# Cross attention of a decoder layer: probabilities normalised before the turn, turned output summed in place, scores a tile ahead, weights stored split

## The reference

```
x = x + self_attention(layernorm(x))
x = x + cross_attention(layernorm(x), ctx)
x = x + ffn(layernorm(x))
```

```
scores  = qh @ kh.T / sqrt(dk)
weights = softmax(scores)
out     = weights @ vh
```

## Time and profile before

| | us |
|---|---|
| median of 3 runs (lowest, highest) | 3618.52 (3617.93, 3620.3) |
| the profiled execution | 3618.95 |
| its span | 3616.8 |
| TensorE busy (share of the span) | 3440.5 (95%) |
| VectorE busy | 1494.1 (41%) |
| ScalarE busy | 1185.0 (33%) |
| GpSimd busy | 1250.3 (35%) |
| mean granted TensorE clock | 0.977 |

### The profile page before, as it was taken

The page is one execution under the profiler, slowest core; times in us unless marked ns, Lnnn a source line. Parts: engine busy times, 40 slices in busy tenths (PEclk is TensorE's granted clock), DMA queues, the critical chain, the costliest instruction groups (busy, mean ns, idle before and its releaser), DMA issues. The chain is left out here.

```text
span 3616.8 us, 49438 instructions
## 1 busy us (share of the span) xinstructions
PE 3440.5 (95%) x18100; PEld 2677.0 (74%) x18100; DVE 1494.1 (41%) x2238; ACT 1185.0 (33%) x1679; POOL 1250.3 (35%) x563
## 2 busy tenths in 40 slices
PE   6999999999999999999999679989979999998999
PEld 5888887888878888878787467767767777763587
DVE  3232332323332232423232446656656665652453
ACT  3232232323233232323222235445444454440110
POOL 4334343434324343434342334434334443320000
PEclk9999999999999999999999889999999999999999
DMA  4323233323333232332221254544555455534032
GB/s 168 106 94 113 89 135 130 115 93 106 127 128 117 93 110 93 128 134 89 85 93 53 108 150 128 173 146 137 156 152 137 129 161 162 141 88 157 35 133 76
DMA packets 137253, 431.16 MB, mean 119 GB/s; under 512 B 24112, under 2 KB 24112, under 8 KB 137144
## 3 DMA queue, kind: packets, MB, share of 16 engines
q1 hardware_dynamic: 131384, 408.58, 35.1%
q10 hardware_dynamic: 5760, 20.97, 1.4%
HBM read 316.21 MB, written 37.75 MB: 98 GB/s over the span
## 5 line engine op out<-in xcount | busy, mean ns | idle before, releaser
L446 POOL TENSOR_TENSOR sa_wl<-sa_wraw,sa_wh 128x1024 fp32r<-128x1024 f32 x192 | 458.2, 2402 | 777.3 <-ACT sa_wh L597 777.3
L53 PE MATMUL sa_u<-sa_ln_xh,sa_wh 128*128 128x512 f32 x1536 | 628.5, 409 | 4.4 <-DVE sa_ln_xl L254 4.4
L54 PE MATMUL sa_u<-sa_ln_xl,sa_wh 128*128 128x512 f32 x1536 | 599.7, 390 | 0.0
L55 PE MATMUL sa_u<-sa_ln_xh,sa_wl 128*128 128x512 f32 x1536 | 599.3, 390 | 0.0
L457 POOL TENSOR_TENSOR sa_pl<-sa_praw,sa_ph 128x1024 fp32r<-128x1024 f32 x128 | 318.0, 2516 | 446.4 <-ACT sa_ph L649 446.4
L53 PE MATMUL sa_pr<-sa_ph,sa_oh 128*128 128x512 f32 x1024 | 428.6, 419 | 0.1
L746 DVE TENSOR_TENSOR sa_acc<-sa_pr,sa_acc 128x512 f32<-128x512 f32 x256 | 176.9, 692 | 569.3 <-PE sa_pr L55 569.3
L54 PE MATMUL sa_pr<-sa_pl,sa_oh 128*128 128x512 f32 x1024 | 400.8, 391 | 0.0
L55 PE MATMUL sa_pr<-sa_ph,sa_ol 128*128 128x512 f32 x1024 | 400.0, 391 | 0.0
L738 DVE TENSOR_TENSOR sa_ol<-sa_o,sa_oh 128x512 fp32r<-128x512 f32 x128 | 88.6, 692 | 718.5 <-ACT sa_oh L661 718.5
L53 PEld LDWEIGHTS sa_u<-sa_ln_xh,sa_wh 128*128 128x128 f32 x1536 | 289.3, 188 | 83.6 <-issue 24.2
(11 more groups left out here) (185 smaller groups left out, 5765.7 us busy)
## 6 DMA issues: line engine op xcount, KB each, us to landing
sa_wraw<-in_wqkv SPq DMA_DIRECT2D x192, 512.0 KB, 3.5
sa_praw<-in_wproj SPq DMA_DIRECT2D x128, 512.0 KB, 3.5
ca_wraw<-w_folded SPq DMA_DIRECT2D x96, 512.0 KB, 3.2
ca_kstack<-ca_kmh SPq DMA_DIRECT2D x256, 128.0 KB, 2.4
ca_wraw<-in_wo SPq DMA_DIRECT2D x33, 512.0 KB, 4.2
ca_kstack<-ca_kml SPq DMA_DIRECT2D x128, 128.0 KB, 2.4
ca_qstack<-ca_qh SPq DMA_DIRECT2D x256, 64.0 KB, 2.5
...
```

The costliest lines, as they stand in the source:

```text
L53: nc.tensor.matmul(out, ah, bh, start=(first and i == 0), stop=False)
L54: nc.tensor.matmul(out, ah, bl, start=False, stop=False)
L55: ins = nc.tensor.matmul(out, al, bh, start=False, stop=(last and i == len(parts) - 1))
L446: nc.gpsimd.tensor_tensor(wl[:, u % 3], wraw[:, u % 3], f32(wh[:, u % 3]), ALU.subtract).then_inc(w_split, 1)
```

## The change

In self-attention the folded weights are stored as two arrays, high and low: `copy_fold` writes the high part and VectorE the low part (`low_fold`), and `store_fold` issues two DMAs. The cross phase loads both straight into `wh` and `wl`; only Wo's slice is still split there.

In the attention the negated, scaled maximum goes to ScalarE as the exp's bias: 8 exps of 128 columns a tile, from the scores' bank, which is free only after the last of them. VectorE sums each half of the slots and inverts the sums (`sums`), GpSimd multiplies (`normal_probs`), and the normalised probabilities are turned. v stands in pairs of slots with zeros between (`VW` = 96), so that the two slots of a pair, one into rows 0 to 15 of a band of 32, the other into rows 16 to 31, are summed in one place by `mix_values`; the result is the output, turned, as `project` wants it. copy_oT, turn_oT, scale_o and turn_o are gone. scores(t) stands before turn_probs(t - 1).

The diff, cut:

```diff
-                        act.wait_ge(fold_stored, m * 16 + 16)
-                    nc.scalar.activation(fold[:, half * HALF:(half + 1) * HALF], v_ps[:], ACT.Copy
-                                         ).then_inc(v_copied, 1)
+                        act.wait_ge(fold_stored, m * 32 + 32)
+                    nc.scalar.activation(foldh[:, half * HALF:(half + 1) * HALF], v_ps[:], ACT.Copy
+                                         ).then_inc(fold_hi, 1)
 
                 def store_fold():
                     if not s.steady:
                         return
                     act.wait_ge(v_copied, v0 + 4)
-                    act.dma_start(tile_of(w_folded, m), fold[:]).then_inc(fold_stored, 16)
+                    act.dma_start(tile_of(w_folded_hi, m), f32(foldh[:])).then_inc(fold_stored, 16)
+                    act.dma_start(tile_of(w_folded_lo, m), f32(foldl[:])).then_inc(fold_stored, 16)
...
+                def low_fold(half):
+                    if not s.steady:
+                        return
+                    dve.wait_ge(fold_hi, m * 2 + (half + 1))
+                    cols = slice(half * HALF, (half + 1) * HALF)
+                    nc.vector.tensor_tensor(foldl[:, cols], v_ps[:], f32(foldh[:, cols]), ALU.subtract
+                                            ).then_inc(v_copied, 1)
...
                 low_o(0)
                 next_moments(0)
+                low_fold(0)
                 low_o(1)
                 next_moments(1)
                 add_projected(0)
+                low_fold(1)
...
-        v = sb("ca_v", [P, TILES * SLOTS, DP])
+        v = sb("ca_v", [P, TILES * PAIRS, VW])
...
-            def weights(n, item, g, skipped=0):
-
-                if not (isinstance(n, int) and n < 0):
-                    sp.wait_ge(w_split, splits(n, item + (-2), skipped))
-                src = {OUT: wo, VALUE: w_folded, KEY: w_folded, QUERY: w_folded}[item]
-                first = {OUT: 0, VALUE: 2 * CH, KEY: CH, QUERY: 0}[item]
-                sp.dma_start(wraw[:, item % 2], tile_of(src, g + first)).then_inc(wraw_loaded[item % 2], 16)
+            def weights(u, g):
+                first = CH * WHICH[u]
+                sp.dma_start(f32(wh[:, u]), tile_of(w_folded_hi, g + first)).then_inc(w_loaded[u], 16)
+                sp.dma_start(f32(wl[:, u]), tile_of(w_folded_lo, g + first)).then_inc(w_loaded[u], 16)
+
+            def next_weights(s, u):
+                if s.nxt:
+                    sp.wait_ge(u_done, s.n * U + (u + 1))
+                    weights(u, s.next_g)
...
-                    weights(s.n + 1, OUT, s.g, 0 if s.nxt else 2)
+                    next_weights(s, 0)
+                    sp.wait_ge(ow_split, s.n + 1)
+                    sp.dma_start(owraw[:], tile_of(wo, s.g)).then_inc(owraw_loaded, 16)
...
-                    if s.nxt:
-                        weights(s.n + 1, VALUE, s.next_g)
+                    next_weights(s, 1)
                 if s.norm:
                     load_context(s.b + 1, range(CRAW, KC))
+                if s.proj:
+                    next_weights(s, 2)
...
+            def out_weights(s):
+                if not s.attn:
+                    return
+                pool.wait_ge(ow_hi, s.m + 1)
+                nc.gpsimd.tensor_tensor(owl[:], owraw[:], f32(owh[:]), ALU.subtract).then_inc(ow_split, 1)
...
+            def normal_probs(s, t):
+                if not s.attn:
+                    return
+                for half in range(2):
+                    pool.wait_ge(inv_done, (s.m * TILES + t) * 2 + (half + 1))
+                    js = slice(half * SH, (half + 1) * SH)
+                    nc.gpsimd.tensor_tensor(probs[:, t % 2, js], probs[:, t % 2, js],
+                                            inv[:, t % 2, js].unsqueeze(2).broadcast_to([P, SH, P]), ALU.mult
+                                            ).then_inc(probs_ready, 1)
...
-                weights(s.n, OUT, 0 if s.proj else 2)
-                if s.proj:
-                    weights(s.n, VALUE)
-                    mask_k(s)
-                if s.nxt:
-                    weights(s.n, KEY)
-                    weights(s.n, QUERY)
+                out_weights(s)
+                normal_probs(s, 0)
+                mask_k(s, kmh, kh)
+                normal_probs(s, 1)
+                mask_k(s, kml, kl)
+                normal_probs(s, 2)
+                normal_probs(s, 3)
...
-                            pe.wait_ge(w_split, [splits(n, KEY - ITEMS), splits(n, QUERY - ITEMS), splits(n, VALUE)][u])
+                            pe.wait_ge(w_loaded[u], n * 32 + 32)
...
-                    pe.wait_ge(s_shifted, m * TILES + (t + 1))
+                    pe.wait_ge(exp_done, (m * TILES + t) * 2 + 2)
...
-                    for j in range(SLOTS):
-                        rows = slice(DP * (j % 4), DP * (j % 4 + 1))
-                        ins = nc.tensor.matmul(o_ps[rows, (j // 4) * P:(j // 4 + 1) * P],
-                                               v[:, t * SLOTS + j], probsT[:, j * P:(j + 1) * P],
-                                               start=True, stop=True)
+                    for w in range(2):
+                        for r in range(PAIRS):
+                            j = 2 * r + w
+                            ins = nc.tensor.matmul(o_ps[DP * r:DP * (r + 1), 0:P],
+                                                   v[:, t * PAIRS + r, DP * w:DP * (w + 1)],
+                                                   probsT[:, j * P:(j + 1) * P], start=(w == 0), stop=(w == 1))
...
-                if s.cross:
-                    turn_x(0)
-                    turn_x(1)
-                    pieces(0)
-                    turn_x(2)
-                    pieces(1)
-                    turn_x(3)
-                    scores(0)
-                else:
-                    scores(0)
-                    pieces(0, 1)
-                turn_v()
+                scores(0)
+                turn_x(0)
+                turn_x(1)
+                pieces(0)
+                turn_x(2)
+                pieces(1)
+                turn_x(3)
                 pieces(2)
                 turn_x(4)
                 pieces(3)
+                turn_v()
                 turn_x(5)
                 pieces(4)
                 turn_x(6)
-                turn_probs(0)
                 pieces(5)
                 turn_x(7)
-                for t in range(1, TILES):
-                    first = 5 * t + 1
-                    scores(t)
-                    mix_values(t - 1)
-                    pieces(first)
-                    turn_oT(t - 1)
-                    pieces(first + 1, first + 2)
-                    turn_o(t - 1)
-                    pieces(first + 3, first + 4)
-                    project(t - 1, 0)
-                    turn_probs(t)
-                    project(t - 1, 1)
+                scores(1)
+                pieces(6, 7)
+                turn_probs(0)
+                pieces(8, 9, 10)
+                mix_values(0)
+                scores(2)
+                pieces(11, 12)
+                project(0, 0)
+                turn_probs(1)
+                project(0, 1)
+                pieces(13, 14)
+                scores(3)
+                mix_values(1)
+                pieces(15, 16)
+                project(1, 0)
+                turn_probs(2)
+                project(1, 1)
+                pieces(17, 18)
+                mix_values(2)
+                pieces(19, 20)
+                project(2, 0)
+                turn_probs(3)
+                project(2, 1)
+                pieces(21)
                 mix_values(3)
...
                 def exps(t):
                     if not s.attn:
                         return
-                    act.wait_ge(s_shifted, m * TILES + (t + 2))
-                    nc.scalar.activation(probs[:, t % 2], probs[:, t % 2], ACT.Exp, scale=CROSS_SCALE
-                                         ).then_inc(probs_ready, 1)
+                    act.wait_ge(negtop_ready, m * TILES + (t + 1))
+                    for half in range(2):
+                        for j in range(half * SH, (half + 1) * SH):
+                            ins = nc.scalar.activation(probs[:, t % 2, j], s_ps[:, j * P:(j + 1) * P], ACT.Exp,
+                                                       scale=CROSS_SCALE, bias=negtop[:, j:j + 1])
+                        ins.then_inc(exp_done, 1)
...
                 set_bias()
+                out_weights()
                 high_x(0, 1, 2, 3)
                 exps(0)
-                high_x(4, 5)
-                out_weights()
-                high_x(6)
+                high_x(4, 5, 6, 7)
+                high_unit(0, kh, km_ready, n * 2)
                 copy_probs(0)
-                high_x(7)
-                copy_oT(0)
-                value_weights()
+                exps(1)
                 high_o(0)
-                high_unit(0, kh, km_ready, n * 2)
-                exps(1)
-                next_weights(KEY, 0)
+                exps(2)
```

(50 more changed lines are left out.)

169 lines of the change are left out of this document (52 added, 117 removed).

## The result

| | before | changed |
|---|---|---|
| median, lowest to highest (us) | 3618.56, 3614.16 to 3621.91, 18 runs | 3624.27, 3616.99 to 3628.81, 18 runs |
| profiled execution (us), its span | 3618.95, 3616.8 | 3624.78, 3623.0 |
| ratio of the times | | 1.0018, 95% interval 1.0011 to 1.0024 |

The change makes the kernel slower by 5.7 us where 29 us were forecast as a gain. By the interval it is slower; in size it stays under the 0.2% (7.2 us) that the prediction took for no difference.

The account below looks back on a forecast made before the run. TensorE's own queue was taken to bound the 1128 us of cross steps. 3618.95 less 19 (ordinary steps), 4 (start) and 6.5 (last step) gave about 3589 us; range 3553 to 3622.

Parts of the forecast that it names:

- What goes on TensorE: Ordinary cross step: removed transposes save 0.33 us a tile, 1.32 a step, and waits of 0.80 go with them.
- The step without waits: Ordinary cross step on TensorE without any wait: 31.9 us, from 33.98 less 1.32 and 0.80.
- What comes in the softmax chain: Delay from scores(t) to turn_probs(t) adds waits summing to 1.35 us; step 33.2, gaining 0.75 us times 25, 19 us.
- The two waits forecast: TensorE in an ordinary step: 0.8 us before turn_probs(0), for GpSimd's multiply, and 0.55 before scores(2), for ScalarE's exps.
- Everything later is ready 0.2 us or more before TensorE comes: Rest of the ordinary step after scores(2): no further wait, for example turn_probs(1) ready at 14.3 against 14.8.
- The rival of VectorE held up by GpSimd: VectorE's reductions held by GpSimd put the second half's sum 0.9 us a step later: 3611 us, chance 0.04.
- The start: First scores(0) of the cross phase comes earlier because weights arrive already split: 4 us gained, 0 to 8.
- The last step: Last cross step, attention alone with no pieces: some 32 us instead of 39, 6.5 gained, 4 to 8.
- Self-attention at 0: Self-attention phase: 48 extra subtractions on VectorE and 12.6 MB of extra stores cost 0; without cover 17 us.
- Norm and cross steps: Six steps that normalise or turn the next block: delays eat what the transposes give, 0 plus or minus 9 us.
- The stacks of q late: Rival: q stacks land after scores(0) wants them, 1.9 us times 31, 59 in all: 3648 us, chance 0.07.
- chain too long: Rival: long exps and multiplies, decisive when scores(0) to turn_probs(0) exceeds 9 us; step 34.7, 3627 us, chance 0.10.

Follow-up runs that it names:

- experiment 8: Kernel of experiment 7 with three transposes of 128 columns a tile put back on TensorE, result unchanged: 3595.47 us, 0.9934 of before.
- experiment 7: Kernel of experiment 2 with sums(0) ahead of place_v on VectorE and exps(1) ahead of copy_probs(0) on ScalarE: 3556.11 us, 0.982 of before.
- experiment 10: Kernel of experiment 7 with scores(2) and a piece ahead of mix_values(0), and the cross step's sums(0) between low_x(5) and low_x(6): 3544.74 us, 0.9794 of before.
- experiment 1: Changed kernel with the negated maxima made on ScalarE instead of VectorE: 3585.25 us, 0.990 of before.
- experiment 2: Changed kernel without a separate negation: the reduction writes the negated maximum, the factor 0.25 sits in the pair mask: 3578.86 us, 0.988 of before.
- experiment 3: Changed kernel with GpSimd's split of the output weights and its two masks of k each cut into two instructions: 3581.31 us, 0.989 of before.
- experiment 4: Changed kernel with VectorE's negation made as a length-1 reduction with negated result, factor 0.25 in the pair mask: 3580.80 us, 0.990 of before.
- experiment 5: Kernel before with only the folded weights stored and loaded split, attention as it was: 3632.84 us, 1.004 of before.
- experiment 6: Kernel of experiment 5 with the output weights' load moved behind the stacks of q in SP's queue: 3625.42 us, 1.002 of before.
- 9: Kernel of experiment 7 with VectorE's order in the norm and cross steps changed, three of four normalisings moved into the next step: 3563.08 us, 0.984 of before.
- 11: Kernel of experiment 10 with the output weights' load moved behind the stacks of q: 3566.42 us, 0.9856 of before.
- 12: Kernel of experiment 10 with GpSimd's context splits kept back until VectorE has normalised all four tiles: 3554.18 us, 0.9828 of before.

## Why the prediction was wrong

By its own steps:

- **What goes on TensorE: right.** 1.32 us a step was forecast for the transposes, 1.37 measured (experiment 8). The step without waits was put at 31.9; experiments 7 and 10 give 31.7 and 31.8. Of the 25 steps that the sum takes as like the one read, 21 are (34.0 us each before); the first of each block takes 35.4 to 37.7.
- **What comes in the softmax chain: here it failed**, at the words "the negated maxima, a tiny operation, at 2.25". They ended at 3.84, and with them fell "scores(1) comes at 5.1 and does not wait": it waited 0.88. I priced the operation by its size, and no row stood behind the price: the bounds of the chain covered the exps and the multiplies, of which I was unsure, and left out the step that I was sure of. The exps and the multiplies came out close: eight exps take 2.18 us where 2.26 were forecast (the estimate of 2.44 by the Trainium skill, "ScalarE: Activation LUTs", What ACT_TABLE_LOAD costs, was too long for this trace), and two multiplies at 2507.23 take 2.07 where 2.2 were forecast. The two waits forecast in place of the real three, 0.8 and 0.55, are the ones that appear in experiments 1 and 2 (0.57 and 0.77, 0.57 and 0.53) once the hold is taken away, and the steps are then 33.28 and 33.00 for the forecast 33.2. The kernel that I predicted is the changed one without the hold, and it came out 4 to 10 us faster than the 3589 forecast.
- **"Everything later is ready 0.2 us or more before TensorE comes": wrong by the same cause.** add_projected(0,0) stood behind the held negation of tile 2. The list of what is ready had turn_probs(1) and mix_values(1), and not the operation behind tops(2) on VectorE. This was 0.82 of the 2.23 us of waits.
- **The rival of VectorE held up by GpSimd** had the right mechanism on the wrong operation. I asked it of the reductions, the large ones, and answered it with rows of one-input operations that are not held. The negation has one input too. The trace of before had the row that decides, the 5.96 us of normalising beside 5.87 of splits; every norm step has it, that of the earlier trace rows too. By it the price is what is left of a GpSimd instruction of 2.4 or 1.9 us. The section of the Trainium skill that the prediction cites ("SBUF — State Buffer", Who interferes with whom) says in the same list that a copy, a cast or a scalar operation within SBUF can take both of VectorE's port pairs and then waits for the whole of a running GpSimd instruction; this trace agrees, with 1.78 and 1.66 us against 0.17. I had used the half of that rule that spoke of two-input operations and reductions.
- **The start**: 4 forecast, 0 to 8; measured 8.7. **The last step**: 6.5 forecast; measured 5.5 by the marks. **Self-attention at 0**: TensorE is busy for 1983.9 us in it for 1984.4, and the cover held.
- **Norm and cross steps, 0 plus or minus 9**: measured 8.9 lost, the end of the range. But with the hold gone the six take 265.3, 267.5, 267.7 and 269.2 us (experiments 1 to 4), for 277.7 in the changed kernel and 268.9 before: the forecast of nothing held for the kernel without the hold, and the 8.9 go with it. Up to 3 us of such a difference can be the gap of 7 to 9 us at the end of the first two cross steps, which varies from kernel to kernel; between the changed kernel and experiment 4 it does not differ. The loss in experiments 5 and 6 is another one, behind the late load of x.
- **The stacks of q late**: no wait for them in the changed kernel's steps. In the attention of before they are late, 0.6 to 1.3 us in ten steps (experiment 5); without the hold scores(0) waits for them in one step, 1.2 to 2.5 us (experiments 1 to 4), and up to 5.7 us in experiment 10.
- **The range** took the long chain and the nothing-gained case for its upper end, 3622. The result is within 3 us of the rival "chain too long", whose point was 9 us from scores(0) to turn_probs(0): it took 8.2 (2509.40 - 2501.20), TensorE having been held at scores(1) already. The sign was that rival's, the mechanism was not.

In sum the hold cost 39 to 45 us by the medians of experiments 1 to 4, or 42 to 48 with each set against the kernel before beside it: it turned a gain of about 40 into a loss of 6. By the marks of experiment 4 some 32 us of it fell in the 21 plain steps (34.54 against 33.02) and 8.5 in the norm and cross steps.

What stays open: why the load of x comes still later in experiment 6 than in experiment 5; a part of the 0.5 us by which the changed kernel's ordinary step, its waits taken off, is longer than that of experiment 10 (34.54 less 2.23 is 32.3, against 31.8); whether the new attention with the weights split in place would be faster still, which was not tried. Beside the step of experiment 2 some 0.3 of the 0.5 can be placed: what follows scores(1) comes 1.14 us later in the changed kernel, where the row names a wait of 0.88, and project(0,1) adds 0.90 for a named 0.82. A wait cost more here than its row says.

## What to carry to other kernels

An operation is not free because it is small: ask of every instruction put into a chain whether it can be held by another engine, and look in the trace for the same kind of operation beside a busy GpSimd, not for one of the same size. A scalar operation within SBUF on VectorE next to long GpSimd instructions is better made as part of a reduction, on ScalarE, or beside shorter GpSimd instructions; each of these took away the whole loss here. And when a step gets shorter, walk every queue once more for what now comes last: three of the twelve edits here only moved a wait (9, 11 and 12), and experiment 7 moved one of two.
